# Routing stage of an attention and mixture-of-experts layer: counts by matmul, gates from the sorted values, the low part of x1 and the token numbers on GpSimd

## The chip, the cores and the metric

The kernel runs on one core of a Trainium2 chip. The metric is the device time of one execution in microseconds (us); less is better. Engines are called TensorE (PE in the profile, its weight loads PEld), VectorE (DVE), ScalarE (ACT), GpSimd (POOL) and SyncE (SP, the queue that issues most transfers).

## What is computed

One layer: causal attention with 16 heads over 2048 tokens of width 512, a projection with W_O, a residual and a layernorm (result x1), and then a feed-forward part with 64 routed experts and one shared expert, again with residual and layernorm. The part that matters here is the routing:

```python
x = _layernorm(x + attention(x))                    # x1: 2048 x 512
logits = xf @ gate_w.T                              # 2048 x 64
scores = softmax(logits)
gate_vals, idx = top_k(scores, 6)
fe = idx.reshape(-1)                                # expert of each pick, token by token
onehot = (fe[:, None] == arange(64)[None, :])
pos = take_along_axis(cumsum(onehot, axis=0) - 1, fe[:, None], axis=1)[:, 0]
keep = pos < CAPACITY                               # 128 slots for each expert
buf = full((64, 128), N).at[fe, pos].set(token)     # which token sits in which slot
xe = xpad[buf]                                      # rows gathered for each expert
h = silu(xe @ w1.T) * (xe @ w3.T); ye = h @ w2.T
routed = sum over the 6 picks of ye[fe, pos] * gate_vals
z = silu(xf @ sw1.T) * (xf @ sw3.T) @ sw2.T         # shared expert
```

## The kernel before

Three programs follow each other: attention (until about 1697 us of the profiled span), `route_and_experts`, and `combine`, which does the last layernorm. Float32 products are made of three passes, hi*hi, hi*lo and lo*hi: each operand is split into a rounded part (ScalarE, `ACTIVATE` with a Copy) and the remainder (a subtraction, written to a tile named `..._lo`).

**The routing stage** goes over 16 tiles of 128 tokens (`TILES`), in a software pipeline written out by hand: each engine has a function `step(i, k)`, and in step k TensorE projects tile k (48 matmuls into `o_ps`, L1385, in pieces of 12, 2 and 2 heads), and between the pieces does the transposes of x1 of tile k-1 (`turn_x1`, L1397), the counts of tile k-2 (`counts`, L1404 and L1405) and the logits of tile k-1 (L1412). Four tiles make a loop body (`NB`), buffers of most tiles are doubled by `k % 2`.

- VectorE, step k: `normalise(k-1)` (L1627 to L1636, with a Newton step from the helper `newton`, L1873 to L1877), `choose(k-2)` (maximum, top 8, indices, the one-hot `pick` of 6x64, L1660, its sum `chosen`, L1664, and that as bf16, L1665), `split_z(k+1)` (`z_lo`, L1614, 128x2048), `route_gates(k-2)` (L1672 to L1676), `split_x1T(k-1)` (`x1T_lo`, L1643), `places(k-2)` (L1685 to L1697: where each pick goes, in `slot`).
- ScalarE, step k: the square root of tile k-1, the exponentials of tile k-2 (L1211), `z_hi` of tile k+1 (L1202), the two copies of the transposes of tile k-1 (`x1T`, L1218, and `x1T_hi`, L1223), one piece of the shared expert's weights (L1231).
- SyncE, step k, in this order: the residual rows `xr` of tile k+1, the store of x1 of tile k-1 (L1091), the load of `z_raw` of tile k+2 (L1073, 1 MB, one buffer), and `store_parts(k-1)`, the stores of `x1T_hi` and `x1T_lo` (L1097), which wait for `t_split`. After step 14 it loads the first two tiles of `sT` (the stored parts again, L1117), which the shared expert needs.
- GpSimd, cycle k: `scatter(k)` waits for `placed` of tile k, issues six indirect transfers (L1008), each of 128 rows of 527 words from `x1` into `gathered_x` at the slots, and waits until all six have landed (`moved`); then it signals `rows_left`. After that `split_shared(k+3)` (L1002, low part of a piece of the shared expert's weights, 128x704 or 128x512) and `load_shared(k+4)` (L997).

`places(k)` on VectorE waits for `rows_left` of tile k-2 before it writes `slot`, and `normalise(k)` for that of tile k-4 before it writes the x1 buffer. The core of `scatter`:

```python
wait_apart(pool, waited, placed, done(0, k))
for n in range(TOPK):
    nc.gpsimd.indirect_dma_start(
        flat, bass.IndirectOffsetOnAxis(ap=slot[:, k % 2, n:n + 1], axis=0), x1[:, k % NB], None,
        bounds_check=last_slot, oob_is_err=False).then_inc(moved, 16)
pool.wait_ge(moved, done(0, k, 16 * TOPK))
pool.sem_inc(rows_left, 1)
```

**The lead stage.** When tile 15 is projected, TensorE goes on with the shared expert on the first four tiles (8 units: `lead_up`, L1466, `lead_down`, L1506, `lead_turn_h`, L1459); `lead_up(0)` waits for `sT`. The rest of the routing (`turn_x1(15)`, `counts(14)`, `logits(15)`, `counts(15)`, on VectorE the `places` of the last two tiles) stands between these units.

**The expert stage** (`body`, four rounds of 16 experts and six shared units) begins with the transposes of the first expert's rows (L1442). SyncE loads them (L1166) only after `rows_left` has reached 16, and after them the weights of the experts.

Of the kernel before, what the change touches and what calls it, by code (L numbers as in the profile page):

```python
# [50 lines left out]
NB = 4  # L51
# [640 lines left out]
def route_and_experts(nc, z_dram, w_o, gate_w, x_rows, w13, w2, s13, s2, sums_dram, x1T_parts, gathered_x):  # L692
# [77 lines left out]
    with ExitStack() as ctx:  # L770
# [23 lines left out]
        with ExitStack() as first:  # L794
# [8 lines left out]
            token = sb("token", [P, TILES], I32, first)  # L803
# [9 lines left out]
            top_e = sb("top_e", [P, 8], stack=first)  # L813
# [3 lines left out]
            chosen = sb("chosen", [P, EXPERTS], stack=first)  # L817
            chosen_bf = sb("chosen_bf", [P, EXPERTS], BF16, first)
            count = sb("count", [P, EXPERTS], stack=first)
            pos_all = sb("pos_all", [P, EXPERTS], stack=first)  # L820
# [7 lines left out]
            ones_bf = sb("ones_bf", [P, P], BF16, first)  # L828
# [73 lines left out]
        l_read = sem("l_read")  # L902
        exp_ready = sem("exp_ready")
# [5 lines left out]
        rows_left = sem("rows_left")  # L909
        ln_chain = sem("ln_chain3")  # L910
# [28 lines left out]
        LN_STEPS = 9  # L939
        CHOOSE_STEPS, GATE_STEPS = 6, 4  # L940
        ROUTE_STEPS = CHOOSE_STEPS + GATE_STEPS + 5
# [35 lines left out]
        def _(pool):  # L977
# [3 lines left out]
            nc.gpsimd.iota(token[:], pattern=[[P, TILES]], base=0, channel_multiplier=1).then_inc(pool_const, 1)  # L981
            pool.wait_ge(pool_step, 2)
# [4 lines left out]
                                    base=0, pattern=[[1, P]], channel_multiplier=-1).then_inc(pool_const, 1)  # L987
            nc.gpsimd.iota(mine_i[:], pattern=[[1, NE]], base=0, channel_multiplier=0).then_inc(pool_const, 1)
# [202 lines left out]
        def _(act):  # L1191
# [152 lines left out]
            act.wait_ge(dve_const, 3)  # L1344
# [29 lines left out]
        def _(pe):  # L1374
# [157 lines left out]
            def lead_down(v):  # L1532
# [3 lines left out]
                if v == 0:  # L1536
# [3 lines left out]
                    pe.wait_ge(t_split, done(0, TILES - 1))  # L1540
# [15 lines left out]
            pe.wait_ge(dve_const, 3)  # L1556
# [33 lines left out]
        def _(dve):  # L1590
# [26 lines left out]
            def normalise(i, k):  # L1617
# [16 lines left out]
                newton(nc, link, small)  # L1634
                assert made[ln_chain] == LN_STEPS, made[ln_chain]
                nc.vector.tensor_scalar(y, y, mv[:, 0:1], small[:, 2:3], ALU.subtract, ALU.mult).then_inc(x1_ready, 1)  # L1636

            def split_x1T(i, k):
                dve.wait_ge(t_hi, done(i, k))
                if exists(i, k - 2):  # L1640

# [411 lines left out]
```

## Time and profile before

| | us |
|---|---|
| median of 3 runs | 2666.51 (2664.92 to 2666.8) |
| the profiled execution | 2663.28 |
| its span, first to last instruction | 2661.6 |
| TensorE busy in the span | 2489.5 (94%) |
| VectorE busy | 1778.8 (67%) |
| ScalarE busy | 1460.7 (55%) |
| GpSimd busy | 274.6 (10%) |

The profile is of one execution; the sum of a prediction is made against its 2663.28 us, which lies 3.2 us under the median. Busy time is that of instructions; a transfer's own time is not in an engine's. An idle time in the rows stands in square brackets or behind the second bar, with what ended it. The routing stage lies between about 1708 and 1942 us, the lead stage between 1942 and 1996 us, the expert stage from there to about 2620 us.

### The profile page before, as it was taken

Reading aid. Unit: us, or ns where it says so; the run is one execution under the profiler, and the core shown is the slowest. Engines: PE = TensorE matmul, PEld = TensorE weight load, DVE = VectorE, ACT = ScalarE, POOL = GpSimd, SP = SyncE. Lnnn points to the kernel's source line nnn. Section 1 sums busy time; section 2 is a strip of 40 time slices with the busy share of each in tenths; the row PEclk is TensorE's granted clock in tenths of the full one; section 3 lists DMA queues with packets and bytes.
Section 4 is the critical chain, followed back from the end, with each engine's and each line's share of the span. In section 5 each row is a group of like instructions: output and inputs, shape, how many; then the busy total and the mean of one; then the engine's idle time right before and its main releaser. Section 6 shows DMA issues by size and latency. Waiting matters only on the chain. (4 is left out here: it accounts for less than half of the span.)

```text
span 2661.6 us, 47883 instructions
## 1 busy us (share of the span) xinstructions
PE 2489.5 (94%) x14304; PEld 2153.4 (81%) x14304; DVE 1778.8 (67%) x3809; ACT 1460.7 (55%) x3254; POOL 274.6 (10%) x221
## 2 busy tenths in 40 slices
PE   6999999999999999999999999798899999999992
PEld 5888888888888888888888888576688988898992
DVE  3665566566466557557466566588868887787885
ACT  3555555455456456456455455444437776677772
POOL 0000000000000000000000000045541222221120
PEclk8999999999999999999999999899999999999996
DMA  6311311310320321311221120467659999999995
GB/s 245 122 49 48 118 49 51 117 50 21 104 94 15 107 79 32 106 54 54 85 79 54 67 78 17 151 225 262 226 155 285 313 300 278 287 307 294 287 314 187
DMA packets 178147, 383.77 MB, mean 144 GB/s; under 512 B 19689, under 2 KB 52585, under 8 KB 167600
## 3 DMA queue, kind: packets, MB, share of 16 engines
q1 hardware_dynamic: 155248, 333.38, 37.2%
q0 software_dynamic: 20288, 42.59, 7.2%
q10 hardware_dynamic: 2304, 4.20, 0.4%
q8 instruction: 132, 2.16, 0.3%
q14 instruction: 175, 1.43, 0.2%
HBM read 282.37 MB, written 106.35 MB: 146 GB/s over the span
## 5 line engine op out<-in xcount | busy, mean ns | idle before, releaser
L403 ACT ACTIVATE pT_hi<-turned 128x512 fp32r<-128x512 f32 (+3 forms) x640 | 331.1, 537 | 311.0 <-PE turned L626 309.6
L497 DVE TENSOR_TENSOR pT_lo<-turned,pT_hi 128x512 fp32r<-128x512 f32 (+3 forms) x640 | 376.6, 606 | 100.9 <-ACT pT_hi L403 99.6
L392 ACT ACTIVATE probs<-bank,neg_max 128x512 f32<-128x512 f32 (+3 forms) x640 | 396.0, 626 | 80.7 <-DVE neg_max L491 76.9
L483 DVE TENSOR_REDUCE max_part<-bank 128x1 f32<-128x512 f32 (+2 forms) x576 | 347.6, 622 | 108.0 <-PE bank L609 99.2
L596 PE MATMUL bank<-x_sb,w_hi 128*128 128x512 f32 x1024 | 327.3, 401 | 20.5 <-ACT ident_bf L367 13.8
L626 PE MATMUL turned<-ident,probs 128*128 128x128 f32 x2176 | 323.6, 275 | 19.6 <-issue 19.1
L626 PEld LDWEIGHTS turned<-ident,probs 128*128 128x128 f32 x2176 | 265.4, 142 | 64.8 <-issue 20.6
L641 PE MATMUL z_ps<-pT_hi,v_hi 128*128 128x512 f32 (+3 forms) x640 | 255.2, 399 | 15.7 <-DVE pT_lo L497 12.9
L609 PE MATMUL bank<-k_lo,q_hi 128*128 128x512 f32 (+2 forms) x640 | 254.0, 397 | 0.0
L1756 DVE TENSOR_TENSOR up_lo<-w_raw,up_hi 128x704 fp32r<-128x704 f32 x262 | 222.4, 887 | 42.0 <-ACT up_hi L1256 41.3
L609 PE MATMUL bank<-k_hi,q_hi 128*128 128x512 f32 (+2 forms) x640 | 250.4, 391 | 0.0
L596 PEld LDWEIGHTS bank<-x_sb,w_hi 128*128 128x128 f32 x1024 | 194.6, 193 | 60.4 <-issue 13.8
L641 PE MATMUL z_ps<-pT_hi,v_lo 128*128 128x512 f32 (+3 forms) x640 | 233.8, 365 | 0.0
L609 PE MATMUL bank<-k_hi,q_lo 128*128 128x512 f32 (+2 forms) x640 | 233.6, 365 | 0.0
L641 PE MATMUL z_ps<-pT_lo,v_hi 128*128 128x512 f32 (+3 forms) x640 | 233.1, 364 | 0.0
L596 PE MATMUL bank<-x_sb,w_lo 128*128 128x512 f32 x512 | 203.0, 396 | 0.0
L585 PE MATMUL bank<-w_hi,x_sb 128*128 128x256 f32 x1024 | 193.2, 285 | 1.7 <-ACT probs L392 1.7
L1256 ACT ACTIVATE up_hi<-w_raw 128x704 fp32r<-128x704 f32 x256 | 189.0, 785 | 2.2 <-DMA w_raw<-in_w 2.2
L978 POOL MEMSET ident<- 128x128 f32 x1 | 0.2, 204 | 1695.2 <-POOLq L146 1695.2
L585 PEld LDWEIGHTS bank<-w_hi,x_sb 128*128 128x128 f32 x1024 | 163.3, 193 | 3.3 <-DVE probs L456 2.1
L1050 POOL DMA_INDIRECT sums_dram<-y_sb,token x64 | 115.4, 1802 | 396.9 <-DMA sums_dram<-y_sb,token 232.9
L468 DVE TENSOR_TENSOR q_lo<-bank,q_hi 128x512 fp32r<-128x512 f32 x64 | 44.3, 692 | 166.1 <-ACT q_hi L376 164.6
(211 smaller groups left out, 5352.4 us busy)
## 6 DMA issues: line engine op xcount, KB each, us to landing
w_raw<-in_w SPq DMA_DIRECT2D x262, 352.0 KB, 5.6
x_sb<-x_parts SPq DMA_DIRECT2D x62, 1024.0 KB, 6.4
w_raw<-in_w SPq DMA_DIRECT2D x129, 256.0 KB, 5.1
rows_in<-gathered_x SPq DMA_DIRECT2D x65, 263.5 KB, 5.4
gathered_x<-empty_row SPq DMA_DIRECT2D x64, 263.5 KB, 9.2
z_dram<-z_sb SPq DMA_DIRECT2D x64, 256.0 KB, 2.9
z_raw<-z_dram SPq DMA_DIRECT2D x16, 1024.0 KB, 5.6
w_raw<-in_w_qkv SPq DMA_DIRECT2D x32, 384.0 KB, 10.2
```

The costliest lines, as they stand in the source:

```text
L392: nc.scalar.activation(probs[:, u % 2, r, kc * CHUNK:kc * CHUNK + used], bank[:, job_at["s", h, c, r, kc] % BANKS, 0:used], ACT.Exp, bias= ...
L403: nc.scalar.activation(pT_sb[0][:, n % TURNS, lo_col:], turned[:, n % TURNS, lo_col:], ACT.Copy).then_inc(turn_hi, 1)
L483: nc.vector.reduce_max(max_part[:, row % ROWS, kc:kc + 1], bank[:, job % BANKS, 0:used], axis=AX_X).then_inc(part_done, 1)
L497: nc.vector.tensor_tensor(pT_sb[1][:, n % TURNS, lo_col:], turned[:, n % TURNS, lo_col:], pT_sb[0][:, n % TURNS, lo_col:].bitcast(F32), AL ...
L585: mark = nc.tensor.matmul(dst[:, t * 2 * DH:(t + 1) * 2 * DH], x_sb[:, a, dt, rows_], w_sb[b][:, dt, 4 * DH:], start=(dt == 0 and (a, b) = ...
L596: mark = nc.tensor.matmul(dst, w_sb[a][:, dt, first:first + DH], x_sb[:, b, dt, :], start=(dt == 0 and (a, b) == PASSES[0]), stop=(dt == D ...
L609: mark = nc.tensor.matmul(dst[:, 0:width], q_sb[a][:, h, r * P:(r + 1) * P], k_sb[b][:, h, kc * CHUNK:kc * CHUNK + width], start=(a, b) == ...
L626: mark = nc.tensor.transpose(turned[:, n % TURNS, r * P:(r + 1) * P], probs[:, u % 2, r, j * P:(j + 1) * P], ident[:])
L641: mark = nc.tensor.matmul(z_ps[:, first * P:], v_sb[a][:, j, h * DH:(h + 1) * DH], pT_sb[b][:, n % TURNS, first * P:], start=(j == 0 and ( ...
L1050: nc.gpsimd.indirect_dma_start(sums_dram, bass.IndirectOffsetOnAxis(ap=token4[:, n:n + 1], axis=0), y_sb[:, n % 2], None, bounds_check=las ...
L1256: nc.scalar.activation(dst_of(0, n % 2, p, up_w, down_w), raw_of(raw, q % SLOTS_RAW, p), ACT.Copy).then_inc(w_hi, 1)
L1756: nc.vector.tensor_tensor(dst_of(1, n % 2, p, up_w, down_w), raw_of(raw, q % SLOTS_RAW, p), dst_of(0, n % 2, p, up_w, down_w).bitcast(F32) ...
```

## The change

Six edits, all in `route_and_experts`:

1. `pick` becomes bf16 and is doubled. TensorE multiplies it directly: six matmuls with `before_bf` (tokens ahead in the tile) and, for the tile before, six with `rest_bf` (its complement: this token and those behind it), all accumulated in one bank `c_ps` that is never cleared. The sum `chosen`, its bf16 copy, the running `count` and `pos_all` go.
2. The gates are the exponentials of the six sorted values `top`, a second small instruction on ScalarE; the product with the one-hot and its sum go.
3. The low part of x1T is subtracted on GpSimd, from `x1T` in SBUF instead of `t_ps` in PSUM: `split_x1T(k + 2)` stands right behind `scatter(k)`. TensorE no longer waits for it before it transposes the next tile; ScalarE waits for it before it writes the buffer again two tiles later.
4. The token numbers are written by an iota on GpSimd ahead of each scatter, no longer copied by VectorE.
5. The Newton step is three instructions, not five.
6. The chain of own waits is shortened to match.

```diff
-            pick = sb("pick", [P, TOPK, EXPERTS], stack=first)
+            pick = sb("pick", [P, 2, TOPK, EXPERTS], BF16, first)
-            c_ps = ps("c_ps", [P, 2, EXPERTS], stack=first)
+            c_ps = ps("c_ps", [P, EXPERTS], stack=first)
...
+            def split_x1T(k):
+                pool.wait_ge(t_hi, done(0, k))
+                pool.wait_ge(t_read, done(0, k))
+                if k >= 2:
+                    pool.wait_ge(t_stored[k % 2], 32 * (k // 2))
+                nc.gpsimd.tensor_tensor(xT_part[1][:, k % 2], x1T[:, k % 2], xT_part[0][:, k % 2].bitcast(F32),
+                                        ALU.subtract).then_inc(t_split, 1)
+
             def scatter(k):
+                if k >= NB:
+                    pool.wait_ge(x1_stored[k % NB], 16 * (k // NB))
                 wait_apart(pool, waited, placed, done(0, k))
+                nc.gpsimd.iota(x1[:, k % NB, TOKEN:TOKEN + 1].bitcast(I32), pattern=[[0, 1]], base=k * P,
+                               channel_multiplier=1).then_inc(token_made, 1)
+                pool.wait_ge(token_made, k + 1)
                 for n in range(TOPK):
...
             for k in range(AHEAD):
                 split_shared(k)
                 load_shared(k + 1)
+                if k:
+                    split_x1T(k - 1)
             for k in range(TILES):
                 scatter(k)
+                if k + 2 < TILES:
+                    split_x1T(k + 2)
...
             def exponentials(i, k):
-                act.wait_ge(l_read, done(i, k))
-                nc.scalar.activation(ex[:], lg_c[:], ACT.Exp, accum_out=small[:, 4:5]).then_inc(exp_ready, 1)
+                act.wait_ge(topped, done(i, k))
+                nc.scalar.activation(ex[:], lg_c[:], ACT.Exp, accum_out=small[:, 4:5])
+                nc.scalar.activation(top_e[:], top[:, 0:TOPK], ACT.Exp).then_inc(exp_ready, 1)
...
                     act.wait_ge(l_ready, done(i, k - 2))
+                    act.wait_ge(t_split, done(i, k - 2))
...
-                    pe.wait_ge(t_split, done(i, k - 1))
+                    pe.wait_ge(t_read, done(i, k - 1))
+                    pe.wait_ge(t_hi, done(i, k - 1))
...
             def counts(i, k):
-                pe.wait_ge(chosen_ready, done(i, k))
                 if exists(i, k - 1):
                     pe.wait_ge(c_read, done(i, k - 1))
-                nc.tensor.matmul(c_ps[:, 0], before_bf[:], chosen_bf[:], start=True, stop=True)
-                nc.tensor.matmul(c_ps[:, 1], ones_bf[:], chosen_bf[:], start=True, stop=True).then_inc(c_ready, 1)
+                    for n in range(TOPK):
+                        nc.tensor.matmul(c_ps[:], rest_bf[:], pick[:, (k - 1) % 2, n], start=False, stop=False,
+                                         skip_group_check=True)
+                pe.wait_ge(chosen_ready, done(i, k))
+                for n in range(TOPK):
+                    mark = nc.tensor.matmul(c_ps[:], before_bf[:], pick[:, k % 2, n], start=not exists(i, k - 1) and n == 0,
+                                            stop=n == TOPK - 1, skip_group_check=True)
+                mark.then_inc(c_ready, 1)
...
             def route_gates(i, k):
-                link(nc.vector.tensor_tensor(pick_pos[:], pick[:], ex[:].rearrange("p (k e) -> p k e", k=1)
-                                             .to_broadcast([P, TOPK, EXPERTS]), ALU.mult))
-                link(nc.vector.reduce_sum(top_e[:, 0:TOPK], pick_pos[:], axis=AX_X))
...
             def places(i, k):
                 dve.wait_ge(c_ready, done(i, k))
-                link(nc.vector.tensor_tensor(pos_all[:], c_ps[:, 0], count[:], ALU.add))
-                nc.vector.tensor_tensor(count[:], c_ps[:, 1], count[:], ALU.add).then_inc(c_read, 1)
...
-                nc.vector.tensor_copy(x1[:, k % NB, TOKEN:TOKEN + 1].bitcast(I32), token[:, bass.ds(t, 1)])
...
             def step(i, k):
                 if exists(i, k - 2):
                     route_gates(i, k - 2)
-                if exists(i, k - 1):
-                    split_x1T(i, k - 1)
                 if exists(i, k - 2):
                     places(i, k - 2)
```

How the change moves instructions on GpSimd, from the first scatter on (`s_up_lo` and `s_down_lo` are pieces of the shared expert's weights, `gathered_x` is the target of the scatter); lines of the new kernel with a plus:

```order
 L997 DMA s_raw<-in_s 128x704
-L1008 DMA gathered_x<-x,slot 8192x527 x6
+L1011 TENSOR_TENSOR x1T_lo<-x1T,x1T_hi 128x512
+L1018 IOTA x 128x1
+L1022 DMA gathered_x<-x,slot 8192x527 x6
+L1011 TENSOR_TENSOR x1T_lo<-x1T,x1T_hi 128x512
 L1002 TENSOR_TENSOR s_up_lo<-s_raw,s_up_hi 128x704
 L997 DMA s_raw<-in_s 128x512
```

Each cycle of GpSimd gets an iota ahead of its six scatters and a subtraction behind them.

VectorE, one step of the loop, before (from the indices of the chosen experts to the end of `places`):

```order
L1659 CAST x<-idx 128x8
L1660 TENSOR_TENSOR pick<-iota_f,x 128x384
L1664 TENSOR_REDUCE chosen<-pick 128x64
L1665 CAST chosen_bf<-chosen 128x64
L1614 TENSOR_TENSOR z_lo<-z_raw,z_hi 128x2048
L1672 TENSOR_TENSOR pick_pos<-pick,ex 128x384
L1674 TENSOR_REDUCE top_e<-pick_pos 128x6
L1675 RECIPROCAL small<-small 128x1
L1676 TENSOR_SCALAR x<-top_e,small 128x6
L1643 TENSOR_TENSOR x1T_lo<-t_ps,x1T_hi 128x512
L1685 TENSOR_TENSOR pos_all<-c_ps,count 128x64
```

And the same place now:

```order
+L1681 CAST x<-idx 128x8
+L1685 TENSOR_TENSOR pick<-iota_f,x 128x384
+L1641 TENSOR_TENSOR z_lo<-z_raw,z_hi 128x2048
+L1698 RECIPROCAL small<-small 128x1
+L1699 TENSOR_SCALAR x<-top_e,small 128x6
+L1707 TENSOR_TENSOR pick_pos<-pick,c_ps 128x384
```

Six of the eleven rows are gone, and the product that finds the place reads `c_ps` itself.

## Rows read from the trace of the kernel before

**Rows 1.** Windows: busy time by engine, granted clock, DMA share, GB/s

```profile
1858.00:1873.00 15.00, 15.00 (x75) 12.25 (x74) 13.00 (x34) 5.40 (x8) 7.35 (x7) 1.00 0.79 301
```

**Rows 2.** Timeline, SyncE: stores of x1, the second and the fifteenth

```profile
1738.36 0.33 SPq L1091 DMA_DIRECT2D sums_dram<-x  x1
...
1936.68 0.34 SPq L1091 DMA_DIRECT2D sums_dram<-x  x1
```

**Rows 3.** Groups of instructions, VectorE: busy us, mean ns, idle before

```profile
L1672 DVE TENSOR_TENSOR pick_pos<-pick,ex 128x384 f32<-128x384 f32 x16 | 14.0, 875 | 0.4 <-ACT ex L1211 0.4
L1664 DVE TENSOR_REDUCE chosen<-pick 128x64 f32<-128x384 f32 x16 | 13.3, 830 | 0.6
L1643 DVE TENSOR_TENSOR x1T_lo<-t_ps,x1T_hi 128x512 fp32r<-128x512 f32 x16 | 11.1, 692 | 2.4 <-ACT x1T_hi L1223 1.3
L1674 DVE TENSOR_REDUCE top_e<-pick_pos 128x6 f32<-128x384 f32 x16 | 8.9, 553 | 0.6
L1665 DVE CAST chosen_bf<-chosen 128x64 bf16<-128x64 f32 x16 | 7.4, 460 | 0.5
```

**Rows 4.** Timeline, GpSimd: start, duration, instruction, idle before it

```profile
1749.85 1.05 POOL L1008 DMA_INDIRECT gathered_x<-x,slot  x1 [1.67 <-DVEq L1698]
1751.20 1.01 POOL L1008 DMA_INDIRECT gathered_x<-x,slot  x1 [0.30 <-issue]
...
1865.11 2.53 POOL L1002 TENSOR_TENSOR s_up_lo<-s_raw,s_up_hi 128x704 fp32r<-128x704 f32 x1 [5.92 <-DMA gathered_x<-x,slot]
...
1879.06 1.66 POOL L1002 TENSOR_TENSOR s_up_lo<-s_raw,s_up_hi 128x704 fp32r<-128x704 f32 x1 [2.81 <-DMA gathered_x<-x,slot]
...
1909.61 1.26 POOL L1002 TENSOR_TENSOR s_down_lo<-s_raw,s_down_hi 128x512 fp32r<-128x512 f32 x1 [2.55 <-DMA gathered_x<-x,slot]
...
1925.87 2.96 POOL L1008 DMA_INDIRECT gathered_x<-x,slot  x1 [0.16 <-issue]
...
1939.48 0.98 POOL L1008 DMA_INDIRECT gathered_x<-x,slot  x1 [4.22 <-DMA gathered_x<-x,slot]
...
1974.12 1.26 POOL L1008 DMA_INDIRECT gathered_x<-x,slot  x1 [2.06 <-DMA gathered_x<-x,slot]
```

**Rows 5.** Groups of instructions, GpSimd: an iota

```profile
L988 POOL IOTA mine_i<- 128x16 int32 x1 | 0.1, 132 | 0.0
```

**Rows 6.** Waits between 1720 and 1941 us: total, times, longest

```profile
POOL s_down_lo L1002 <- DMA gathered_x<-x,slot: 29.6, 6, 6.9
...
POOL s_up_lo L1002 <- DMA gathered_x<-x,slot: 24.2, 5, 6.6
...
PE c_ps L1404 <- DVE chosen_bf L1665: 14.9, 9, 2.3
```

**Rows 7.** Timeline, TensorE: a pair of counts, the logits, lead and expert stage begin

```profile
1939.90 0.20 PE L1404 MATMUL c_ps<-chosen_bf,before_bf 128*128 128x64 bf16 x1
1939.94 0.19 PE L1405 MATMUL c_ps<-chosen_bf,ones_bf 128*128 128x64 bf16 x1
...
1942.25 0.41 PE L1466 MATMUL h_even<-s_up_hi,sT 128*128 128x352 f32 x1
...
1996.50 1.06 PE L1442 MATMUL t_odd<-ident,rows_in 128*128 128x128 f32 x4
```

**Rows 8.** Timeline, SyncE: loads of z_raw, of sT and of the expert rows

```profile
1852.07 0.35 SPq L1073 DMA_DIRECT2D z_raw<-z_dram  x1
...
1866.24 0.35 SPq L1073 DMA_DIRECT2D z_raw<-z_dram  x1
...
1931.16 1.84 SPq L1117 DMA_DIRECT2D sT<-x1T_parts  x4
...
1983.03 0.33 SPq L1166 DMA_DIRECT2D rows_in<-gathered_x  x1
```

**Rows 9.** Timeline, VectorE: the low part of z under that GpSimd issue

```profile
1925.68 2.28 DVE L1614 TENSOR_TENSOR z_lo<-z_raw,z_hi 128x2048 fp32r<-128x2048 f32 x1
```

**Rows 10.** Transfers by line: KB each, median us from issue to landing

```profile
rows_in<-gathered_x SPq DMA_DIRECT2D x65, 263.5 KB, 5.4
```

More of the change, by code:

```diff
@@ L812, in route_and_experts @@
             top = sb("top", [P, 8], stack=first)
-            top_e = sb("top_e", [P, 8], stack=first)
+            top_e = sb("top_e", [P, TOPK], stack=first)
             idx = sb("idx", [P, 8], U32, first)
-            pick = sb("pick", [P, TOPK, EXPERTS], stack=first)
+            pick = sb("pick", [P, 2, TOPK, EXPERTS], BF16, first)
             pick_pos = sb("pick_pos", [P, TOPK, EXPERTS], stack=first)
[L817 to L820, printed above, removed]
             slot = sb("slot", [P, 2, TOPK], U32, first)
@@ L827, in route_and_experts @@
             before_bf = sb("before_bf", [P, P], BF16, first)
-            ones_bf = sb("ones_bf", [P, P], BF16, first)
+            rest_bf = sb("rest_bf", [P, P], BF16, first)
         s_up.append([sb(f"s_up_{n}1", [P, DT, 2 * INTER], F32R) for n in ("hi", "lo")])
@@ L980, in _ @@
             nc.gpsimd.iota(iota_i[:], pattern=[[1, EXPERTS]], base=0, channel_multiplier=0).then_inc(pool_const, 1)
-            nc.gpsimd.iota(token[:], pattern=[[P, TILES]], base=0, channel_multiplier=1).then_inc(pool_const, 1)
-            pool.wait_ge(pool_step, 2)
+            nc.gpsimd.memset(rest_bf[:], 1.0).then_inc(pool_step, 1)
+            pool.wait_ge(pool_step, 3)
             nc.gpsimd.affine_select(out=ident[:], in_=ident[:], compare_op=ALU.not_equal, fill=1.0,
@@ L1633, in normalise @@
                 link(nc.vector.reciprocal(small[:, 2:3], small[:, 0:1]))
-                newton(nc, link, small)
+                link(nc.vector.scalar_tensor_tensor(small[:, 6:7], small[:, 2:3], small[:, 2:3], small[:, 1:2], ALU.mult, ALU.mult))
+                link(nc.vector.tensor_scalar(small[:, 7:8], small[:, 6:7], -0.5, 1.5, ALU.mult, ALU.add))
+                link(nc.vector.tensor_tensor(small[:, 8:9], small[:, 7:8], small[:, 2:3], ALU.mult))
                 assert made[ln_chain] == LN_STEPS, made[ln_chain]
[L1636 to L1640, printed above, removed]
-                    dve.wait_ge(t_stored[k % 2], i * (32 * NB // 2) + 32 * (k // 2))
-                nc.vector.tensor_tensor(xT_part[1][:, k % 2].rearrange("p t n -> p (t n)"), t_ps[:],
-                                        xT_part[0][:, k % 2].rearrange("p t n -> p (t n)").bitcast(F32),
-                                        ALU.subtract).then_inc(t_split, 1)
+                nc.vector.tensor_scalar(y, y, mv[:, 0:1], small[:, 8:9], ALU.subtract, ALU.mult).then_inc(x1_ready, 1)
             def choose(i, k):
@@ L1655, in choose @@
                 wait_apart(dve, waited, l_read, done(i, k))
-                link(nc.vector.max(top[:], lg_c[:]), apart=True)
-                link(nc.vector.max_index(idx[:], top[:], lg_c[:]))
+                nc.vector.max(top[:], lg_c[:]).then_inc(topped, 1)
+                wait_apart(dve, waited, topped, done(i, k))
+                link(nc.vector.max_index(idx[:], top[:], lg_c[:]), apart=True)
                 idx_f = x1[:, k % NB, CHOICES:CHOICES + 8]
                 link(nc.vector.tensor_copy(idx_f, idx[:]))
-                link(nc.vector.tensor_tensor(
-                    pick[:], iota_f[:].rearrange("p (k e) -> p k e", k=1).to_broadcast([P, TOPK, EXPERTS]),
+                if exists(i, k - 1):
+                    dve.wait_ge(c_ready, done(i, k - 1))
+                nc.vector.tensor_tensor(
+                    pick[:, k % 2], iota_f[:].rearrange("p (k e) -> p k e", k=1).to_broadcast([P, TOPK, EXPERTS]),
                     idx_f[:, 0:TOPK].rearrange("p (k e) -> p k e", e=1).to_broadcast([P, TOPK, EXPERTS]),
-                    ALU.is_equal))
-                link(nc.vector.reduce_sum(chosen[:], pick[:].rearrange("p k e -> p e k"), axis=AX_X))
-                nc.vector.tensor_copy(chosen_bf[:], chosen[:]).then_inc(chosen_ready, 1)
+                    ALU.is_equal).then_inc(chosen_ready, 1)
+                dve.wait_ge(chosen_ready, done(i, k))
+                dve.sem_inc(route_chain, 1)
+                made[route_chain] += 1
                 assert made[route_chain] == CHOOSE_STEPS, made[route_chain]
@@ L1823, in _ @@
             nc.vector.memset(eps[:], EPS).then_inc(dve_const, 1)
-            nc.vector.memset(ones_bf[:], 1.0).then_inc(dve_const, 1)
-            nc.vector.memset(count[:], 0.0).then_inc(dve_const, 1)
-            dve.wait_ge(dve_const, 3)
+            dve.wait_ge(dve_const, 1)
             split_z(0, 0)
@@ L1868, in _ @@
             shared_result(BODIES, NU - 1, True, False)
-def newton(nc, step, s):
-    step(nc.vector.tensor_tensor(s[:, 6:7], s[:, 2:3], s[:, 2:3], ALU.mult))
-    step(nc.vector.scalar_tensor_tensor(s[:, 7:8], s[:, 6:7], -0.5, s[:, 1:2], ALU.mult, ALU.mult))
-    step(nc.vector.tensor_scalar(s[:, 8:9], s[:, 7:8], 1.5, None, ALU.add))
-    step(nc.vector.tensor_tensor(s[:, 9:10], s[:, 8:9], s[:, 2:3], ALU.mult))
-    step(nc.vector.tensor_copy(s[:, 2:3], s[:, 9:10]))
 def combine(nc, sums_dram, out_rows):
```

31 lines of the change are left out of this document (15 added, 16 removed).

## The prediction

> **What bounds the kernel now.** The edits lie in the routing stage, 234 of 2662 us, so I read its windows first, then each engine's pace, then the waits. In a window of 15 us, about one tile, VectorE is busy 13.0 us and TensorE can be busy throughout [rows 1]. The pace is that of the stores of x1: from the second, 1738.36, to the fifteenth, 1936.68, there are 13 steps of 15.25 us [rows 2]. TensorE waits for the counts' input, 14.9 us in nine waits [rows 6], so VectorE sets the pace. That is what the change attacks.
>
> Then GpSimd, which looks idle by its busy time. Its timeline says otherwise. The first scatter waits for VectorE (1.67 us, at 1749.85); the twelfth begins at 1925.87 [rows 4]. These eleven cycles take 176.0 us, 16.0 each, and the reader should look at what stands in the brackets: after the first, no cycle waits for VectorE. A cycle is six issues, a wait until they have landed, a subtraction, a load. The wait for landing is 29.6 + 24.2 = 53.8 us in eleven cycles [rows 6], 4.9 us each, between 2.55 and 6.9. So GpSimd runs a chain of its own that is no faster than VectorE's, and lags behind it. VectorE doesn't feel this, since `places(k)` wants only the scatter of tile k-2.
>
> The end of the stage is the third thing. The lead stage begins at 1942.25, the first transposes of expert rows stand at 1996.50 [rows 7], while the last scatter had landed by 1983.03, when SyncE issued the load of those rows [rows 8]. Such a load takes 5.4 us to land [rows 10], so GpSimd has about 8 us to spare at this end.
>
> **The change, part by part.**
>
> VectorE loses the product and sum of the gates (875 and 553 ns), `chosen` and its cast (830, 460), `x1T_lo` (692), [rows 3]: 3.4 us per tile. The additions for `count` and `pos_all`, two Newton steps and the token copy are small, of at most 64 columns; I take the five at 0.9 together (an estimate: the cast of 64 columns, at 0.46, bounds one from above). With some 0.04 us of gap for each of ten, 4.7 us: VectorE would need 15.25 - 4.7 = 10.6 us per tile.
>
> TensorE gets 12 small matmuls for 2. Their rows last 0.20 us, but they start 0.04 us apart [rows 7]; ten more cost 0.4 us if they stream, at most 2.0 if not. I take 0.4, by the starts. Without its waits on VectorE TensorE's step is 48 projections, 4 transposes, 8 logits: about 12.4 us by a window in which it never waits (75 matmuls in 15 us, 62 to a step [rows 1]), now 12.8. If nothing else bound, the stage would gain 13 x (15.25 - 12.8) = 32 us.
>
> ScalarE gets one more exponential of six columns; it has idle time, and this is hidden by `z_lo` on VectorE. Without cover it would cost under half a microsecond per tile.
>
> GpSimd gets the subtraction, 128x512, for which the nearest row is 1.26 us [rows 4], and the iota, 0.13 us [rows 5], with a wait for its own semaphore; between dependent steps of its chain stand 0.30 us [rows 4], so 0.4 for both. Together 1.7 us in each of the cycles 0 to 13, 0.4 in the last two. They stand in a chain that has no slack, so they are not hidden: over eleven cycles 11 x 1.7 = 18.7 us.
>
> What can give some of it back is the wait for landing. In the short cycle that ends at 1879.06 `z_raw` was sent off at 1866.24, 10 us ahead of the last issue's end (landing 2.81); in the long one that ends at 1865.11 at 1852.07, 7 us ahead (landing 5.92) [rows 4, 8]. The 1 MB load ahead of the scatters or amid them makes the difference. Now `t_split` comes from GpSimd, and `store_parts` waits for it: behind it in SyncE's queue are `xr`, the store of x1 and the next `z_raw`. They all leave in one burst right after the subtraction, five issues of 0.35 us [rows 8]: `z_raw` some 3 us after `rows_left`. The last of the six issues ends 1.3 + 1.7 + 0.9 + 0.4 + 7.7 = 12 us after it (the two subtractions, the load, the iota, the scatters), so `z_raw` is 9 us ahead. I take 4.0 us of landing, between the two rows and nearer the short one; ends 2.55 and 4.9. Then a cycle is 16.0 + 1.7 - 0.9 = 16.8 us.
>
> Once GpSimd is two tiles behind, VectorE waits for `rows_left` in `places`, and TensorE behind it for x1. The stage then runs at 16.8, not at 15.25. Before that TensorE and VectorE are ahead, which buys nothing, since only the end of the chain counts.
>
> The end: scatter 11 had landed at 1939.48 [rows 4]. It lands at 1939.5 + 11 x 0.8 = 1948.3. **A new dependence** starts here: the loads of `sT` left at 1931.16 [rows 8], before that scatter had landed; now they stand in SyncE's queue behind the stores of tile 13's parts, hence behind the subtraction that follows scatter 11. That is 1948.3 + 1.3 for the subtraction + 0.8 for two stores' issue + 5 for the loads = 1955.4. The lead stage began at 1942.25 and then sat 1.1 us for VectorE, which goes: 1955.4 - 1943.35 = **12 us** later. The last scatter, 1983.0 + 8.8 + 4 x 0.4 + 2 x 1.3 = 1996.0, and the rows' landing at 2001.4 stay under the transposes, now at 2008.5. The expert stage is unchanged and moves as a whole.
>
> Sum: 2663.3 + 12 = 2675.3 for an execution like the profiled one. The median lies 3.2 us above it: 2678.5. With landing at 2.55 the cycle is 15.35 and scatter 11 lands 7 us earlier than before; the lead stage then begins 4 us earlier, at the median 2662.5. At 4.9 the cycle is 17.7 and it begins 22 us later: 2688.5.
>
> One rule is to be weighed. Under a `z_lo` of 1925.68 to 1927.96 an issue on GpSimd took 2.96 us where others take 0.98, and a 128x704 subtraction took 2.53 us at one place, 1.66 at another [rows 4, 9]. The Trainium skill, SBUF — State Buffer, section Who interferes with whom, states that a VectorE instruction with two SBUF inputs and a GpSimd instruction that reads SBUF exclude each other for a whole instruction. That speaks against this change; by it the new subtraction would at worst wait out a `z_lo` of 2.28 us each time, 11 x 2.28 = 25 us on top of my sum; that is the third rival below. My sum goes by 1.26 us, since the subtraction now follows `rows_left`, when VectorE stands in `places` or `normalise`, which read PSUM.
>
> **Rivals.**
>
> *Faster: the landing shrinks.* If the loads run so far ahead that only the floor is left (2.06 us at 1974.12 [rows 4]), a cycle is 16.0 - 2.8 + 1.7 = 14.9, less some 0.9 for issues stretched as at 1925.87: 14.0, above TensorE's 12.8. Scatter 11 lands 22 us earlier, at 1917.5, and the lead stage begins 7.1 us after it, at 1924.6, 18.7 us earlier: 2648. For it: the bytes per tile are the same and fewer things collide. Against it: in eleven cycles no landing was under 2.55 us, and DMA is at 0.79 of its share already [rows 1]. It decides at a mean landing of 2.9 us: below, the change gains.
>
> *No difference.* GpSimd's longer cycle is just paid for by shorter landings (about 3 us), or the lead stage overlaps better than I think: 2666.5, within 5.
>
> *Much slower: the port.* Each new subtraction meets a `z_lo` or is met by one, and costs more than its 1.26 us, as the longer one did: 0.9 more in the row [rows 4], a whole `z_lo` of 2.28 at most [rows 9]: 10 to 25 us on top, 2688 to 2703; half way, 2696. The queue could add to it: `z_raw` now leaves two tiles' work later, and `z_hi` may come to wait for it.
>
> *The change doesn't relieve VectorE.* Its removed instructions are in the order of the new program gone, so I give this nothing.
>
> **How the numbers follow.** My forecast, 2672 to 2690: 0.58. The port, 2688 to 2703: 0.10. No difference: 0.15. Faster: 0.17. A measurement of this kernel tells about 0.2%, 5.3 us, from no change; with the part of each case that falls on either side: faster 0.17, within 0.2% 0.15, slower 0.68. The range leaves out some 0.12 below and 0.06 above: 2657 to 2695.
>
> **What would show it.** In the new profile GpSimd's groups have `x1T_lo` at about 1.3 us, sixteen times, and an iota at 0.13 before each scatter. The scatters start 16.8 us apart (16.0 before). VectorE gets idle time, ended by the landing of `gathered_x` or by GpSimd, before the instruction that writes `slot`, some 4 us a tile or more. SyncE issues the stores of x1T's parts later than the next tile's x1 is ready, in one burst with `z_raw`. The lead stage begins near 1955, behind a wait of several us for `sT`. It is wrong if scatters come under 15.7 us apart, if the wait for landing falls under 3 us, or if TensorE's step turns out at 13 us with VectorE still waiting for nothing.

## The result and the profile after

The changed kernel takes 2671.26 us (median of 20 runs, 2662.85 to 2683.04), the kernel before 2663.28 us in runs beside it (20 runs). The ratio is **1.0036, 95% interval 1.0025 to 1.0047**: slower by some 10 us (9.6 by the ratio, 8.0 between the medians), under half a percent. The forecast was 2678.5 us, 12 us above the 2666.51 us it started from. The profiled execution took 2672.62 us, 9.3 more than the one of before.

VectorE lost work: 1778.8 us busy before, now 1731.0, which is 3.0 us per tile. The window that answers to [rows 1], in the changed kernel:

```profile
1858.00:1873.00 15.00, 13.27 (x73) 10.59 (x73) 9.93 (x21) 6.87 (x10) 10.90 (x10) 1.00 0.66 245
```

VectorE fell from 13.0 to 9.93 us, but TensorE fell too, from 15.0 to 13.27: both now wait. GpSimd rose from 7.35 to 10.90. Its timeline in the changed kernel (start, duration, instruction, idle before it), which answers to [rows 4]: the first issues of the first and the twelfth scatter, the end of the twelfth, and one whole cycle.

```profile
1749.65 1.07 POOL L1022 DMA_INDIRECT gathered_x<-x,slot  x1 [0.29 <-POOL x L1018]
...
1850.95 1.28 POOL L1011 TENSOR_TENSOR x1T_lo<-x1T,x1T_hi 128x512 fp32r<-128x512 f32 x1 [4.27 <-DMA gathered_x<-x,slot]
1852.18 3.73 POOL L1002 TENSOR_TENSOR s_up_lo<-s_raw,s_up_hi 128x704 fp32r<-128x704 f32 x1
1856.22 0.59 POOL L997 DMA_DIRECT2D s_raw<-in_s  x1 [0.30 <-POOL s_up_lo L1002]
1856.82 0.15 POOL L1018 IOTA x<- 128x1 int32 x1
1857.25 1.02 POOL L1022 DMA_INDIRECT gathered_x<-x,slot  x1 [0.28 <-POOL x L1018]
...
1863.70 0.98 POOL L1022 DMA_INDIRECT gathered_x<-x,slot  x1 [0.30 <-issue]
1866.94 1.29 POOL L1011 TENSOR_TENSOR x1T_lo<-x1T,x1T_hi 128x512 fp32r<-128x512 f32 x1 [2.26 <-DMA gathered_x<-x,slot]
...
1935.34 1.13 POOL L1022 DMA_INDIRECT gathered_x<-x,slot  x1 [0.28 <-POOL x L1018]
...
1945.94 1.28 POOL L1011 TENSOR_TENSOR x1T_lo<-x1T,x1T_hi 128x512 fp32r<-128x512 f32 x1 [1.88 <-DMA gathered_x<-x,slot]
```

(1935.34 - 1749.65) / 11 = **16.9 us** per cycle, 16.0 before, 16.8 forecast. In the cycle shown GpSimd waits for nothing but the landing (2.26 us) between one subtraction and the next; its other gaps are 0.3 us: a chain without slack. Its parts, from the groups of GpSimd's instructions of the changed kernel (busy us, mean ns, idle before and what ended it):

```profile
L1022 POOL DMA_INDIRECT gathered_x<-x,slot x96 | 101.5, 1057 | 29.1 <-issue 24.4 <-POOL x L1018 4.8
L1011 POOL TENSOR_TENSOR x1T_lo<-x1T,x1T_hi 128x512 fp32r<-128x512 f32 x16 | 24.2, 1512 | 51.7 <-DMA gathered_x<-x,slot 43.3 <-ACT x1T_hi L1244 8.4
L1002 POOL TENSOR_TENSOR s_up_lo<-s_raw,s_up_hi 128x704 fp32r<-128x704 f32 x8 | 21.2, 2646 | 37.5 <-ACT s_up_hi L1252 37.5
```

The subtraction takes 1.51 us in the mean, not 1.26. The weights' low part (128x704) takes 2.65, and was 2.17. Added up from the timelines over the eleven cycles alone, one cycle spends:

| us per cycle | before | after |
|---|---|---|
| six issues and the gaps beside them | 8.47 | 8.16 |
| iota | | 0.15 |
| wait for the landing | 4.89 | 3.93 |
| subtraction of x1T | | 1.61 |
| weights' low part | 1.80 | 2.21 |
| load, with its gap | 0.81 | 0.82 |
| sum | 16.0 | 16.9 |

The 3.93 us hold two waits that the profile puts down to ScalarE's `x1T_hi` (8.4 us together).

Both subtractions meet VectorE on the way. In the cycle shown, VectorE's timeline beside GpSimd's rows of 1850.95 and 1852.18 has:

```profile
1851.30 3.08 DVE L1641 TENSOR_TENSOR z_lo<-z_raw,z_hi 128x2048 fp32r<-128x2048 f32 x1 [0.96 <-ACT z_hi L1220]
...
1854.49 1.46 DVE L1699 TENSOR_SCALAR x<-top_e,small 128x6 f32<-128x6 f32 x1
```

`z_lo` takes 3.08 us instead of 2.28, GpSimd's subtraction of the weights 3.73 instead of 1.66 [rows 4], and VectorE's instruction of six columns 1.46 instead of 0.23. `z_lo` ends 2.15 us behind the first subtraction, the second subtraction 1.53 us behind `z_lo`, and the six columns end with it, as if each had waited for the one before.

Who waits for that chain is told by the waits of the changed kernel between 1720 and 1960 us (total, times, longest), as [rows 6]:

```profile
ACT s_down_hi L1252 <- DMA s_raw<-in_s: 47.0, 6, 10.3
DVE small L1660 <- ACT small L1225: 42.3, 16, 5.9
ACT s_up_hi L1252 <- DMA s_raw<-in_s: 38.8, 4, 11.0
POOL x1T_lo L1011 <- DMA gathered_x<-x,slot: 38.2, 11, 6.9
...
PE t_ps L1419 <- DVE x L1666: 21.7, 8, 4.6
```

And by one place on ScalarE and VectorE (timeline):

```profile
1844.27 0.79 ACT L1252 ACTIVATE s_up_hi<-s_raw 128x704 fp32r<-128x704 f32 x1 [10.51 <-DMA s_raw<-in_s]
...
1846.37 0.29 ACT L1225 ACTIVATE small<-mv,eps 128x1 f32<-128x1 f32 x1
```

```profile
1846.77 0.16 DVE L1660 RECIPROCAL small<-small 128x1 f32<-128x1 f32 x1 [5.93 <-ACT small L1225]
```

GpSimd loads the piece of the shared weights late; ScalarE, in order, waits 10.51 us for it ahead of the square root; VectorE waits 5.93 for the root; TensorE for x1. The same ScalarE wait was there before (24.2 + 23.3 us in nine), but ended while VectorE was still busy. The expected wait of VectorE for `rows_left` didn't come.

TensorE's granted clock fell with its waits. Windows over the same 145 us, before and then after:

```profile
1760.00:1905.00 145.00, 125.48 (x591) 100.61 (x591) 123.59 (x319) 60.05 (x81) 79.44 (x71) 0.98 0.73 254
```

```profile
1760.00:1905.00 145.00, 126.71 (x659) 102.45 (x659) 91.22 (x213) 59.33 (x88) 90.58 (x82) 0.93 0.66 231
```

The clock was 0.98 of full speed before and 0.93 after, in the mean. The forecast had no term for it, and no run separates what it costs.

The end of the stage, answering to [rows 7, 8]: TensorE's counts and the starts of the lead and expert stages, then SyncE's loads.

```profile
1948.84 0.35 PE L1428 MATMUL c_ps<-pick,rest_bf 128*128 128x64 bf16 x6
1949.02 0.34 PE L1432 MATMUL c_ps<-pick,before_bf 128*128 128x64 bf16 x6
1949.20 0.48 PE L1406 MATMUL o_ps<-wo_hi,z_hi 128*128 128x512 f32 x1
...
1953.22 0.40 PE L1495 MATMUL h_even<-s_up_hi,sT 128*128 128x352 f32 x1 [1.55 <-issue]
...
2006.58 1.06 PE L1471 MATMUL t_odd<-ident,rows_in 128*128 128x128 f32 x4
```

```profile
1948.17 1.92 SPq L1135 DMA_DIRECT2D sT<-x1T_parts  x4
...
1991.67 0.33 SPq L1184 DMA_DIRECT2D rows_in<-gathered_x  x1
```

Twelve counts start within 0.36 us. The lead stage begins at 1953.2; before it ran on from 1943.35, so 9.9 later, and the expert rows follow 10.1 later. That covers the whole loss of the profiled execution. The row of 1953.22 names no releaser; I put its 1.55 us down to `sT`, whose four loads left from 1948.17 on.

### The profile page after: what moved, and what is told of

Same layout as the page of the kernel before. It is cut to its first block and busy times, and to the rows that moved or that the text cites. A ratio compares the mean times of both kernels' runs of the same rounds, so it can differ in the third digit from the quotient of the medians.

```text
span 2671.0 us, 48062 instructions
## 1 busy us (share of the span) xinstructions
PE 2499.3 (94%) x14458; PEld 2163.3 (81%) x14458; DVE 1731.0 (65%) x3647; ACT 1460.8 (55%) x3270; POOL 296.9 (11%) x254
## 5 line engine op out<-in xcount | busy, mean ns | idle before, releaser
L596 PE MATMUL bank<-x_sb,w_hi 128*128 128x512 f32 x1024 | 327.4, 402 | 20.6 <-ACT ident_bf L367 14.1
L596 PEld LDWEIGHTS bank<-x_sb,w_hi 128*128 128x128 f32 x1024 | 194.7, 193 | 60.5 <-issue 14.1
```

Of the source, the lines that this page charges most:

```text
L596: mark = nc.tensor.matmul(dst, w_sb[a][:, dt, first:first + DH], x_sb[:, b, dt, :], start=(dt == 0 and (a, b) == PASSES[0]), stop=(dt == D ...
```

## The experiments

**Theory A:** GpSimd's chain (scatter, landing, subtraction, weights, load) sets the pace after the change. **Theory B:** ScalarE's wait for `s_raw` ahead of the root is the cause by itself. **Theory C:** the loads of `sT` behind the last stores are. A cycle below is the distance of first issues from the first to the twelfth scatter, over 11. Cycles and starts of the lead stage come from the one profiled execution of a run. It lies 10 to 11 us above the run's median in three runs (ScalarE's order, the token numbers back, and both additions back with the late wait) and 7 us in the move alone, so small differences of these figures say little.

### The subtraction back on VectorE

```diff
-                if k + 2 < TILES:
-                    split_x1T(k + 2)
...
+                if exists(i, k - 1):
+                    split_x1T(i, k - 1)
```

Out of GpSimd's loop, into VectorE's `step`, from `t_ps` as before; TensorE waits for `t_split` again.

> The change without its third part: the low part of x1T is subtracted by VectorE again, the other edits stay. Theory A (GpSimd's chain of scatter, landing, subtractions and load sets the pace): the scatters come 16.9 - 1.5 = 15.4 us apart or a little less, the lead stage begins about 15 us earlier than with the change, 2655 to 2660 us, ratio to before 0.997 to 1.000. Theory B (the new wait of ScalarE for s_raw ahead of the square root is the cause by itself, whatever GpSimd's load): the time stays within 3 us of the change's, ratio 1.003. Theory C (the order in SyncE's queue, sT behind the last parts): the lead stage's wait goes, 2 us and no more, ratio 1.002.

2654.4 us, **0.9963 [0.994, 0.9986]**; cycle 15.6; the lead stage begins at 1935.77. VectorE's wait for the root falls from 42.3 us to 29.6 (15.5 put down to ScalarE, 14.1 in four waits without a named releaser). Edit 3 alone turns the rest of the change, a gain of 0.4%, into a loss: it costs 1.0036 - 0.9963 = 0.7%, 19 us.

### The subtraction done twice on GpSimd

```diff
+                                        ALU.subtract).then_inc(token_made2, 1)
+                pool.wait_ge(token_made2, k + 1)
+                nc.gpsimd.tensor_tensor(xT_part[1][:, k % 2], x1T[:, k % 2], xT_part[0][:, k % 2].bitcast(F32),
                                         ALU.subtract).then_inc(t_split, 1)
```

> The change with the new subtraction on GpSimd done twice, each time with the same result. Theory A: 1.3 to 1.6 us more in each of the cycles 0 to 11, scatters 18.3 us apart, 15 to 18 us slower than the change, ratio to before 1.009 to 1.010. Theory B: the same way if ScalarE's wait comes from the late load, so this run cannot part A and B. Theory C: no more than one subtraction, 1.5 us, ratio 1.004.

2700.89 us, **1.0139 [1.0115, 1.0162]**; cycle 19.3, so 2.4 us more per dose. GpSimd's groups, of the whole execution:

```profile
L1015 POOL TENSOR_TENSOR x1T_lo<-x1T,x1T_hi 128x512 fp32r<-128x512 f32 x16 | 28.8, 1798 | 1.4
L1012 POOL TENSOR_TENSOR x1T_lo<-x1T,x1T_hi 128x512 fp32r<-128x512 f32 x16 | 24.9, 1557 | 60.8 <-DMA gathered_x<-x,slot 56.4 <-ACT x1T_hi L1248 4.4
```

The sign is as A has it, the size is not: a dose is 1.80 us, not 1.3, and the landing waits grow too (56.4 us against 43.3). The lead stage also began behind an idle time of 7.17 us, put down to `sT`, and then ran slowly. Windows of that place:

```profile
1976.00:1983.00 7.00, 0.00 (x0) 0.00 (x0) 4.65 (x12) 1.58 (x2) 5.58 (x7) 0.67 0.65 194
1983.00:1989.00 6.00, 5.88 (x21) 5.91 (x22) 0.00 (x0) 0.00 (x0) 3.94 (x4) 0.53 0.34 120
```

After 7 us without a matmul the granted clock was 0.53, near the lower of TensorE's two levels (1.2 and 2.4 GHz). So this run's loss isn't the chain's alone.

### GpSimd waits for the landing last

```diff
-                pool.wait_ge(moved, done(0, k, 16 * TOPK))
-                pool.sem_inc(rows_left, 1)
+            def landed(k):
+                pool.wait_ge(moved, done(0, k, 16 * TOPK))
+                pool.sem_inc(rows_left, 1)
...
                     load_shared(k + AHEAD + 1)
+                landed(k)
```

The wait and the signal leave `scatter` and stand behind the subtractions and the load.

> The change, but GpSimd waits for the landing of its six scatters only after the two subtractions and the load, which until now stood behind that wait. Theory A: the landing of some 4 us is covered by 3.9 us of work, scatters come about 13 us apart, TensorE becomes the bound at 12.8 to 13, the lead stage begins near 1922 us instead of 1953, 2640 to 2648 us, ratio to before 0.992 to 0.995. Theory B: also faster, as the load goes out earlier, but no further than ScalarE's wait of some 4 us a tile allows. Theory C: unchanged within 3 us.

2647.83 us, **0.9941 [0.9924, 0.9958]**; cycle 14.6; lead stage at 1929.59. The same work, with two subtractions and the load under the landing instead of behind it, is 1.0036 - 0.9941 = 0.95% faster. It shows that GpSimd's order of work is in the path, as A says; B had forecast a gain too, so this run doesn't part them. The cycle and the bound were missed: not 13 us but 14.6, and TensorE still waits for VectorE's x1, 6.0 us in seven. The timeline, VectorE and then GpSimd, shows something else too:

```profile
1850.02 3.41 DVE L1667 TENSOR_TENSOR small<-small 128x1 f32<-128x1 f32 x1
```

```profile
1850.45 1.31 POOL L1011 TENSOR_TENSOR x1T_lo<-x1T,x1T_hi 128x512 fp32r<-128x512 f32 x1
1851.70 1.70 POOL L1002 TENSOR_TENSOR s_up_lo<-s_raw,s_up_hi 128x704 fp32r<-128x704 f32 x1
```

A product of one column with one column, 0.16 us elsewhere, ends when GpSimd's second subtraction does. In nine tiles a small step of the layernorm takes 1.9 to 3.4 us this way, ahead of x1. The Trainium skill, SBUF — State Buffer, section Who interferes with whom, has a VectorE instruction with two SBUF inputs contend with a GpSimd instruction that reads SBUF; by that rule, the trace agrees.

### ScalarE splits the weights behind the root and the exponentials

```diff
                     exponentials(i, k - 2)
+                if 0 < k <= SHARED_PARTS * NP:
+                    split_shared(k - 1)
...
-                if k < SHARED_PARTS * NP:
-                    split_shared(k)
```

> The change, but ScalarE does its piece of the shared weights (which waits for s_raw) behind the next tile's square root and exponentials instead of ahead of them. Theory A: the wait of VectorE for the square root (42 us in all) goes, but GpSimd's chain stays at 16.9 us a cycle and VectorE waits for rows_left ahead of slot instead; the time stays within 3 us of the change's, ratio 1.003. Theory B: the wait is the cause, the tile's pace falls from 16.9 towards 13 to 14 us, 20 us or more faster, ratio to before 0.995 or less. Theory C: unchanged.

2676.08 us, **1.0044 [1.0027, 1.0061]**; cycle 17.2. VectorE's wait for the root is down to 3.9 us (and 1.7 without a named releaser), and nothing is gained. The waits:

```profile
DVE z_lo L1641 <- ACT z_hi L1220: 60.8, 14, 6.5
POOL x1T_lo L1011 <- DMA gathered_x<-x,slot: 53.7, 12, 6.0
...
ACT z_hi L1220 <- DMA z_raw<-z_dram: 26.2, 12, 3.8
...
PE l_ps L1441 <- ACT x1T L1239: 18.8, 9, 3.1
```

The wait moved from the root to `z_lo` and `x1T`, not to `slot` as A had it. ScalarE's `z_hi` now waits for `z_raw`, whose load stands in SyncE's queue behind the stores that wait for GpSimd's subtraction. **B falls**: the place of ScalarE's split only chooses through whom the lateness is passed on.

### The subtraction on GpSimd, in the kernel before

```diff
                 scatter(k)
+                if k + 2 < TILES:
+                    split_x1T(k + 2)
...
-                if exists(i, k - 1):
-                    split_x1T(i, k - 1)
```

The move alone, with its waits, as the only edit to the kernel before.

> The kernel before with the third part of the change alone: the low part of x1T on GpSimd, nothing else. Theory A: 1.3 to 1.6 us more in each cycle of GpSimd's chain, scatters 17.0 to 17.5 us apart instead of 16.0, 10 to 16 us slower than before, ratio 1.003 to 1.006, though VectorE has 0.7 us less to do. Theory B (VectorE's load sets the pace and the moved subtraction relieves it): 11 x 0.7 = 8 us faster, ratio 0.997.

2691.27 us, **1.0096 [1.0073, 1.012]**; cycle 17.6. The move alone costs 26 us, more than the whole change: the other edits give back some 16. A wins, with the size again missed from below: 10 to 16 us had been expected. The cycle grew by 1.6 us, which is what the subtraction takes there (1.65 in the mean of the eleven cycles); the wait for the landing, 4.8 with two waits for ScalarE in it, gave nothing back.

### The token numbers back on VectorE

```diff
-                nc.gpsimd.iota(x1[:, k % NB, TOKEN:TOKEN + 1].bitcast(I32), ...).then_inc(token_made, 1)
-                pool.wait_ge(token_made, k + 1)
...
+                nc.vector.tensor_copy(x1[:, k % NB, TOKEN:TOKEN + 1].bitcast(I32), token[:, bass.ds(i * NB + k, 1)])
```

> The change without its fourth part: the token numbers are copied by VectorE again, no iota stands ahead of the scatters. Theory A: 0.4 us less in each cycle, 16.5 us apart instead of 16.9, 4 to 5 us faster than the change, ratio to before 1.001 to 1.002. Theory B: nothing, or slower by VectorE's 0.2 us a tile, ratio 1.003.

2670.24 us, **1.0025 [1.001, 1.0041]**, against 1.0036 [1.0025, 1.0047]: the intervals overlap; cycle 17.1, not 16.5. No effect of the iota is settled. By the timelines it adds little: 0.15 us and the gap ahead of the first issue, which was there before.

### The late wait in the kernel before

```diff
-                pool.wait_ge(moved, done(0, k, 16 * TOPK))
-                pool.sem_inc(rows_left, 1)
...
                     load_shared(k + AHEAD + 1)
+                landed(k)
```

> The kernel before with one edit: GpSimd waits for the landing of a tile's scatters only after the subtraction and the load that stood behind that wait. Theory A with VectorE next: GpSimd's cycle could fall to 13, but VectorE needs 14.3 to 15.25 us a tile here, so the gain is 0 to 8 us, ratio 0.997 to 1.000, and now GpSimd waits for placed. If GpSimd's chain alone set the pace before: about as much as in the change's case, 20 us, ratio 0.992.

2664.11 us, **1.0002 [0.9986, 1.0018]**; cycle 16.2. The waits:

```profile
POOL gathered_x L1008 <- DMA gathered_x<-x,slot: 64.3, 13, 6.7
...
PE t_ps L1400 <- DVE x L1639: 13.8, 9, 2.9
```

GpSimd doesn't wait for `placed`, as had been expected, but for the landing as long as before (64.3 us in thirteen; 29.6 + 24.2 + 10.6 = 64.4 in thirteen in the kernel before), although some 2.3 us of work now stand ahead of that wait. The rows land 7.0 us behind the last issue, 4.9 before: in five of eleven cycles `z_raw` left only 4.5 us ahead of it. So the landing isn't a length that work can simply cover; it moves with a load that follows VectorE's pace. VectorE waits for ScalarE 6.0 us in fourteen and 4.8 in two, and TensorE for VectorE. So **VectorE was the bound before**, as far as waits tell, with GpSimd held to it through the landing. Relief of GpSimd alone is worth nothing here; relief of VectorE alone gave 0.4% in the first experiment.

### Both additions back on VectorE, and the late wait

The edits of the first, the sixth and the third experiment together.

> The change with the low part of x1T and the token numbers on VectorE again, and the late wait for the landing. VectorE needs about 11.9 us a tile, GpSimd 7.7 issues + the landing of 4 to 5 us, TensorE 12.8 to 13. Theory A: TensorE sets the pace, 13 to 14 us a tile against 14.6 in the run with the late wait alone; 2638 to 2646 us, ratio 0.991 to 0.994. Rival: the landing is the bound (transfers at their full rate), then 14.6 stays and the ratio is 0.994 as there.

2640.98 us, **0.991 [0.9888, 0.9932]**; cycle 14.7; lead stage at 1928.74 (in an execution of 2651.91 us). Faster than both kernels, but TensorE still waits for VectorE, 4.8 us for x1, so it doesn't set the pace alone.

### Both additions back, no late wait

> The changed kernel with both GpSimd additions taken back (subtraction and token numbers on VectorE), the wait for landing where it was. If the two effects add up as measured singly (0.9963 with the subtraction back, against 1.0036 for the whole change; tokens back 1.0025), GpSimd's cycle is 15.2 to 15.6 us and the ratio 0.994 to 0.9965. If the iota's place ahead of the scatters costs nothing, the ratio is that of the subtraction back alone, 0.9963, and the cycle 15.6.

2651.74 us, **0.9951 [0.9934, 0.9969]**; cycle 15.5. Not to be told from the subtraction back alone (0.9963, 15.6). The late wait gives 0.4% on top of it.

### The subtraction back, the late wait, the iota kept

> The changed kernel with the subtraction on VectorE and the late wait for landing, token numbers still on GpSimd. Beside the version with tokens on VectorE too (0.991, cycle 14.7): if the iota stands in the chain, the cycle is 0.3 to 0.5 us longer and the ratio 0.992 to 0.993; if VectorE and TensorE are the bound once the wait for landing has been moved, the cycle and the ratio are the same, 0.991 within the interval.

2628.62 us, **0.9872 [0.9847, 0.9896]**; cycle 13.65; lead stage at 1915.32. It was expected no faster than its sibling with the tokens on VectorE (0.991). Windows of this kernel, then of the sibling:

```profile
1858.00:1873.00 15.00, 15.00 (x86) 12.46 (x84) 12.10 (x32) 7.38 (x15) 9.89 (x12) 1.00 0.88 324
```

```profile
1858.00:1873.00 15.00, 13.55 (x83) 10.82 (x80) 11.77 (x27) 7.12 (x11) 8.90 (x8) 1.00 0.82 277
```

Here **TensorE never waits**, in this window nor in the 145 us around it:

```profile
1760.00:1905.00 145.00, 145.00 (x818) 120.25 (x818) 115.72 (x281) 75.41 (x111) 89.77 (x95) 1.00 0.82 286
```

It is the bound at last, at full clock (1.00, against 0.93 in the changed kernel), and the cycle is near the 12.8 us that the prediction gave its step. Where the sibling loses shows on its VectorE and GpSimd (timelines), and this kernel's VectorE below:

```profile
1853.18 2.70 DVE L1652 TENSOR_SCALAR x<-x,mv,small 128x512 f32<-128x512 f32 x1
```

```profile
1853.86 1.72 POOL L1004 TENSOR_TENSOR s_up_lo<-s_raw,s_up_hi 128x704 fp32r<-128x704 f32 x1
```

```profile
1857.68 0.63 DVE L1655 TENSOR_SCALAR x<-x,mv,small 128x512 f32<-128x512 f32 x1
```

The last step of the layernorm, which TensorE's transposes wait for, is held until GpSimd's subtraction ends, in five tiles of the sibling, for 2.1 to 2.75 us each. Here it isn't; a cast of eight columns behind it is held instead (mean 0.63 us, 0.26 in the sibling), and nobody waits for that at once. The same section of the Trainium skill names `tensor_scalar` and casts among the operations that can take the port pair shared with GpSimd for a whole instruction; that both kinds are held beside GpSimd's subtraction agrees with it.

### An idle iota on GpSimd, tokens on VectorE

```diff
                 wait_apart(pool, waited, placed, done(0, k))
+                nc.gpsimd.iota(idle[:], pattern=[[0, 1]], base=k * P, channel_multiplier=1).then_inc(token_made, 1)
+                pool.wait_ge(token_made, k + 1)
```

> The version with subtraction and token numbers on VectorE and the late wait (0.991), with one edit: GpSimd writes an iota into an unused tile ahead of each scatter and waits for it, 0.7 us that do nothing. If the copy of the token numbers on VectorE is what made that version slower than its sibling with the iota (0.9872), this one is slower than both or equal, 0.991 to 0.993, with GpSimd's cycles at 14.7 us or more. If it was the moment at which GpSimd's subtraction of the weights meets the last step of the layernorm on VectorE (2.7 us instead of 0.55 there), the added 0.7 us moves it out of the way: the ratio falls to 0.987 to 0.989, the mean of that layernorm step from 1.23 to about 0.6 us, and the cycle to about 13.7 us.

2639.65 us, **0.9906 [0.9887, 0.9926]**; cycle 14.4; the layernorm step still 1.05 us in the mean (1.14 without the idle iota). 0.7 us of delay didn't bring the faster version back.

### The faster version once more, beside it

> The version with the subtraction on VectorE, token numbers on GpSimd and the late wait, once more on the same chip as the one with the idle iota: 0.9872 within its interval, 0.985 to 0.990, if the first result holds; 0.991 if that chip or that hour made it.

2632.84 us, **0.988 [0.9856, 0.9904]**. The first result holds; the layernorm step is 0.57 us in the mean. Its lead stage begins at 1915.94, that of the one with the idle iota at 1922.22, 6.3 us apart. The stretched layernorm steps of the latter (2.31, 2.71, 2.78 and 2.15 us against 0.55) come to 7.8 us. So the collision is of the size of the difference, and what counts is which instruction it hits: the casts held in the faster one (0.69 us in the mean) cost VectorE about as much. That the copy of the tokens on VectorE decides whether it happens fits the four runs, but was not isolated: the faster versions also have GpSimd wait for the store of x1 ahead of a scatter. It stays open.

## Why the prediction was right, and where it wasn't

The forecast, 12 us slower, came out at 8 to 10, and the mechanism it named, a longer chain on GpSimd, is the one that the experiments bear out. The 2671.26 us lie 7 us under the forecast of 2678.5 and just under its main case of 2672 to 2690; 3 of the 7 are the starting point, 2666.51 us of three runs, where twenty gave 2663.28. By its steps:

- **VectorE relieved, and nothing of it seen in the time: right, with a size missed.** Its busy time fell by 3.0 us per tile, not by the 4.3 worked out (3.4 + 0.9). Without the moved subtraction the other edits do gain 0.4%, GpSimd's cycle being 15.6 us then; the working had given them nothing.
- **TensorE's 0.4 us for ten more counts: right.** Twelve take 0.36. Its step of 12.8 us, never reached in the changed kernel, was approached in the version where nothing else bound (13.65 per cycle).
- **GpSimd's cycle 16.8: measured 16.9,** by errors that cancel, which is luck. The landing, taken at 4.0 us, is 3.93 in the table above. The subtraction, priced at 1.26 us, took 1.61 in these cycles, and the weights' low part grew by 0.4, which had been given nothing: together 0.76 us a cycle that the sum left out. It was left out on the ground that VectorE would stand in `places` or `normalise`; in the cycle shown it stood in `z_lo`. Against that the iota cost about 0.1 us, not 0.4 (its 0.15 stand where a gap was), and the issues themselves were 0.3 shorter: between 1740 and 1960 us four of them began under a `z_lo`, eight in the kernel before. So the rival of the port was in part true, at 0.76 x 11 = 8 us (an estimate).
- **The landing set by how far ahead `z_raw` leaves: borne out as a reading.** In the cycle above it left at 1854.58, 10.1 us ahead of the last issue's end, and the landing took 2.26; in the one that ends at 1850.95 it was 7.7 us ahead and the landing took 4.27. The prediction had put 9 us; the cycles after the first have 7.1 to 10.2, 8.6 in the mean. No run moved `z_raw` alone.
- **The place of the new wait: wrong.** I had VectorE wait for `rows_left` in `places`. It waits for the square root (42.3 us in sixteen waits), which stands on ScalarE behind a split that waits for GpSimd's late load. The step that failed looked for who waits for `rows_left` and forgot who waits for `s_raw`. The pace was right all the same, since either wait hands on GpSimd's.
- **The end: right but for its size.** Scatter 11 landed at 1945.94, not 1948.3; the last of before had been long (an issue of 2.96 us and 4.22 of landing [rows 4]), which my 11 x 0.8 kept. The lead stage follows 7.3 us behind it, 7.1 forecast. The 1.55 us put down to `sT` are all that C could be worth, a small part of the 9.9. The last scatter's rows stayed hidden.
- **The rivals.** "Faster" needed a landing under 2.9 us; it was 3.93. The port, priced as 10 to 25 us on top of the sum, is there with about 8, paid for by the shorter terms. In the second dose it shows again: 1.80 us for a subtraction of 1.3, in a cycle longer by 2.4.

## What to carry to other kernels

An engine with 10% of busy time can be a bound: read its timeline for the wait that follows each of its own transfers, and price an edit there at its full length. Before work is moved to it, place its wait for the landing behind the work that doesn't need it; here that was worth 0.4 to 0.95% once VectorE had been relieved, and nothing before. Check first that the landing doesn't simply move along, as it did in the kernel before. A subtraction on GpSimd holds small VectorE instructions too; look which of them a third engine waits for.

## What the runs showed of the hardware, unexpected

- A VectorE product of 128x1 took 3.41 us while two GpSimd subtractions ran back to back (1.31 and 1.70 us): the length of the GpSimd work counts, not that of the instruction held.
- A 128x512 `TENSOR_SCALAR` from SBUF to SBUF took up to 2.78 us instead of 0.55 beside one GpSimd subtraction.
- An issue of an indirect transfer on GpSimd is held by VectorE's `z_lo`, a subtraction with both inputs in SBUF. In the kernel before, between 1740 and 1960 us, eight issues began under a `z_lo`; they took 1.92 to 3.00 us and all ended 0.84 to 0.88 us behind it, and no other took over 1.5. With the late wait there it was twelve of twelve. So the 2.96 us of [rows 4] is `z_lo`'s 2.28 [rows 9] waited out, and one more reason why issues and landings shift when the order of work does.
- In the kernel before the rows of a scatter landed 12.3 to 13.1 us after the 1 MB load had been issued in seven of eleven cycles (7.4, 9.8, 11.3 and 13.7 in the others), whether the last issue of the scatter ended 6 or 10 us behind that load. It looks as if both drain together; no run took the load away.
